# Tile 1's x is split on ScalarE and VectorE, and two weight pieces earlier, in a nine-expert MoE and adapter kernel

## What is computed

```python
# layer 0: eight routed experts and one shared expert (D=128, F=512)
g = einsum('bsd,edf->ebsf', x, Wg);  u = einsum('bsd,edf->ebsf', x, Wu)
expert_outs = einsum('ebsf,efd->ebsd', silu(g) * u, Wd)
shared = einsum('bsf,fd->bsd', silu(x @ Sg) * (x @ Su), Sd)
x = x + (1 - sg) * einsum('be,ebsd->bsd', gates, expert_outs) + sg * shared
# layer 1: an adapter chosen by the sequence's language, and a layer norm
h = relu(x @ W1[lang] + b1[lang])
y = x + h @ W2[lang] + b2[lang]
x = x + layernorm(y) * gamma[lang] + beta[lang]
```

## Time and profile before

| | |
|---|---|
| median of 3 runs | 296.86 us (296.78 to 297.94) |
| the profiled execution, its own time | 297.13 us |
| its span in the profile | 295.3 us |
| granted TensorE clock, mean | 0.996 |
| PE busy | 290.9 us, 99% |
| DVE busy | 267.9 us, 91% |
| ACT busy | 231.0 us, 78% |
| POOL busy | 18.8 us, 6% |

### The profile page before, as it was taken

The page is one execution under the profiler, slowest core; times in us unless marked ns, Lnnn a source line. Parts: engine busy times, 40 slices in busy tenths (PEclk is TensorE's granted clock), DMA queues, the critical chain, the costliest instruction groups (busy, mean ns, idle before and its releaser), DMA issues.

```text
span 295.3 us, 5098 instructions
## 1 busy us (share of the span) xinstructions
PE 290.9 (99%) x1515; PEld 145.7 (49%) x1515; DVE 267.9 (91%) x584; ACT 231.0 (78%) x515; POOL 18.8 (6%) x32
## 2 busy tenths in 40 slices
PE   8999999999999999999999999999999999999995
PEld 4444444444444444444444444444444444588883
DVE  4999999998989898988989999999999999977795
ACT  6998878788878787877897788887878876667771
POOL 3200201100000000000001010001100011000011
PEclk9999999999999999999999999999999999999998
DMA  7973110244000000000011001010001110000001
GB/s 205 373 322 109 51 66 20 60 119 114 3 2 0 2 0 0 0 2 1 1 23 25 18 9 39 12 25 21 18 0 39 26 19 10 2 36 3 0 2 36
DMA packets 17940, 13.39 MB, mean 45 GB/s; under 512 B 11486, under 2 KB 15994, under 8 KB 17914
## 3 DMA queue, kind: packets, MB, share of 16 engines
q1 hardware_dynamic: 17482, 12.86, 14.5%
q10 hardware_dynamic: 432, 0.21, 0.2%
HBM read 11.23 MB, written 1.05 MB: 42 GB/s over the span
## 4 chain that ended last, share of the span: by engine, by line
PE 98%; DVE 1%; POOL 0%; POOLq 0%; issue 0%; DVEq 0%
PE up_ps L445 11%; PE gate_ps L396 10%; PE moe_ps L468 10%; PE moe_ps L471 10%; PE up_ps L437 10%; PE moe_ps L469 10%; PE up_ps L440 10%; PE gate_ps L397 10%; PE gate_ps L402 10%; PE moe_ps L512 1%; PE adapt_ps L480 0%; DVE w_lo L689 0%; PE gate_ps L411 0%; PE moe_ps L452 0%; PE x_ps L497 0%; PE gate_ps L414 0%
## 5 line engine op out<-in xcount | busy, mean ns | idle before, releaser
L588 ACT ACTIVATE silu<-gate_ps 128x512 f32<-128x512 f32 (+1 forms) x160 | 88.5, 553 | 46.1 <-PE gate_ps L402 44.4
L705 DVE SCALAR_TENSOR_TENSOR hidden<-silu,up_ps 128x512 f32<-128x512 f32 (+1 forms) x160 | 101.2, 633 | 19.7 <-PE up_ps L445 12.0
L711 DVE TENSOR_TENSOR h_lo<-hidden,h_hi 128x512 f16<-128x512 f32 (+1 forms) x159 | 103.8, 653 | 0.2
L593 ACT ACTIVATE h_hi<-hidden 128x512 f16<-128x512 f32 (+1 forms) x159 | 92.4, 581 | 8.9 <-DVE hidden L705 8.1
L445 PE MATMUL up_ps<-gx_hi,w_lo 128*128 128x512 f16 (+1 forms) x160 | 57.2, 358 | 0.1
L437 PE MATMUL up_ps<-gx_hi,w_hi 128*128 128x512 f16 (+1 forms) x160 | 57.3, 358 | 0.0
L440 PE MATMUL up_ps<-gx_lo,w_hi 128*128 128x512 f16 (+1 forms) x160 | 57.2, 358 | 0.0
L469 PE MATMUL moe_ps<-h_hi,w_lo 128*128 128x512 f16 (+1 forms) x159 | 56.9, 358 | 0.0
L468 PE MATMUL moe_ps<-h_hi,w_hi 128*128 128x512 f16 (+1 forms) x159 | 56.9, 358 | 0.0
L471 PE MATMUL moe_ps<-h_lo,w_hi 128*128 128x512 f16 (+1 forms) x159 | 56.9, 358 | 0.0
L396 PE MATMUL gate_ps<-x_hi,w_hi 128*128 128x512 f16 (+1 forms) x158 | 56.5, 358 | 0.0
(11 more groups left out here) (95 smaller groups left out, 154.7 us busy)
## 6 DMA issues: line engine op xcount, KB each, us to landing
w_full<-weights SPq DMA_DIRECT2D x8, 768.0 KB, 9.0
affine_sb<-affine SPq DMA_DIRECT2D x16, 128.0 KB, 2.9
x_full<-xT SPq DMA_DIRECT2D x3, 256.0 KB, 8.4
x<-x_blocks SPq DMA_DIRECT2D x48, 16.0 KB, 1.8
out_dram<-result SPq DMA_DIRECT2D x3, 256.0 KB, 2.0
w_full<-weights SPq DMA_DIRECT2D x4, 128.0 KB, 3.2
w_full<-w2b SPq DMA_DIRECT2D x24, 16.0 KB
w_full<-weights SPq DMA_DIRECT2D x1, 256.0 KB, 3.9
```

What stands on the lines that cost most here:

```text
L588: nc.scalar.activation(silu_slot(n), gate_ps[n % 2][:, 0:STEPS[n][4]], ACT.Silu, scale=1.0 / W_SCALE).then_inc(silu_ready, 1)
L593: nc.scalar.activation(h_slot(h_hi, n), hidden_slot(n), ACT.Copy).then_inc(h_hi_ready, 1)
L705: nc.vector.scalar_tensor_tensor(out=hidden_slot(n), in0=silu_slot(n), scalar=HIDDEN_RESCALE * (W_SCALE if n < WHOLE_STEPS else 1), in1=up ...
L711: nc.vector.tensor_tensor(h_slot(h_lo, n), hidden_slot(n), h_slot(h_hi, n), ALU.subtract).then_inc(h_lo_ready, 1)
```

## The change

x of tile 1 is no longer split by GpSimd. ACT makes its `x_hi` in step 1, after two gx_hi and ahead of silu(2); DVE makes its `x_lo` in step 2, after the low part of piece 4 and ahead of h_lo(1). PE waits for `x_lo_ready` in place of `x_rest_ready` ahead of gate(4). The high and low parts of piece 3 are made ahead of silu(0) and hidden(0) in place of behind them. GpSimd makes the coefficients of experts 1 to 7 directly after those of expert 0, as soon as their gates are loaded, and then splits tiles 2 and 3 as before.

```diff
-X_AFTER = {1: 3, 2: lo_count(2, 2), 3: lo_count(3, 2)}
+X_AFTER = {2: lo_count(2, 2), 3: lo_count(3, 2)}
...
-                if t > 0 and e == 0 and f == 0:
-                    pe.wait_ge(x_rest_ready, t)
+                if t == 1 and e == 0 and f == 0:
+                    pe.wait_ge(x_lo_ready, 3)
+                if t > 1 and e == 0 and f == 0:
+                    pe.wait_ge(x_rest_ready, t - 1)
...
                 if n == 0:
                     first_weight_hi(2)
+                    first_weight_hi(3)
                 silu_of(n)
-                if n == 0:
-                    first_weight_hi(3)
                 if n in (1, 2):
                     gated_x_hi(1, 2 * n - 2)
                     gated_x_hi(1, 2 * n - 1)
+                if n == 1:
+                    nc.scalar.activation(cols(x_hi, 1, N), cols(x_full, 1, N), ACT.Copy).then_inc(x_hi_ready, 1)
...
                 if n == 0:
                     first_weight_lo(2)
+                    first_weight_lo(3)
                 hidden_of(n)
                 for j, (_, _, _, at) in enumerate(JOBS):
                     if n == at:
                         moe_out(j)
-                if n == 0:
-                    first_weight_lo(3)
...
                 if n == 2:
                     first_weight_lo(4)
+                    dve.wait_ge(x_hi_ready, 3)
+                    nc.vector.tensor_tensor(cols(x_lo, 1, N), cols(x_full, 1, N), cols(x_hi, 1, N),
+                                            ALU.subtract).then_inc(x_lo_ready, 1)
...
-            for t in range(1, TILES):
+            pool.wait_ge(gates_loaded, 16)
+            nc.gpsimd.tensor_tensor(coef[:, B:(NE - 1) * B].rearrange("p (e b) -> p e b", b=B),
...
+                                    ALU.mult).then_inc(coef_ready, 1)
+            for t in range(2, TILES):
                 pool.wait_ge(x_loaded[t - 1], 16)
-                if t > 1:
-                    pool.wait_ge(w_lo_ready, X_AFTER[t])
+                pool.wait_ge(w_lo_ready, X_AFTER[t])
                 nc.gpsimd.tensor_copy(cols(x_hi, t, N), cols(x_full, t, N)).then_inc(x_rest_hi_ready, 1)
-                pool.wait_ge(x_rest_hi_ready, t)
-                if t == 1:
-                    pool.wait_ge(w_lo_ready, X_AFTER[t])
+                pool.wait_ge(x_rest_hi_ready, t - 1)
                 nc.gpsimd.tensor_tensor(cols(x_lo, t, N), cols(x_full, t, N), cols(x_hi, t, N),
                                         ALU.subtract).then_inc(x_rest_ready, 1)
```

More of the change, by code:

```diff
@@ L879, in _ @@
             nc.gpsimd.tensor_scalar(coef[:, (NE - 1) * B:], shared_in, X_SCALE, None, ALU.mult)
-            for t in range(1, TILES):
+            pool.wait_ge(gates_loaded, 16)
+            nc.gpsimd.tensor_tensor(coef[:, B:(NE - 1) * B].rearrange("p (e b) -> p e b", b=B),
+                                    gates_in[:, 2 * B:].rearrange("p (e b) -> p e b", b=B),
+                                    rest[:, :].rearrange("p (o b) -> p o b", o=1).to_broadcast([P, NE - 2, B]),
+                                    ALU.mult).then_inc(coef_ready, 1)
+            for t in range(2, TILES):
                 pool.wait_ge(x_loaded[t - 1], 16)
-                if t > 1:
-                    pool.wait_ge(w_lo_ready, X_AFTER[t])
+                pool.wait_ge(w_lo_ready, X_AFTER[t])
                 nc.gpsimd.tensor_copy(cols(x_hi, t, N), cols(x_full, t, N)).then_inc(x_rest_hi_ready, 1)
-                pool.wait_ge(x_rest_hi_ready, t)
-                if t == 1:
-                    pool.wait_ge(w_lo_ready, X_AFTER[t])
+                pool.wait_ge(x_rest_hi_ready, t - 1)
                 nc.gpsimd.tensor_tensor(cols(x_lo, t, N), cols(x_full, t, N), cols(x_hi, t, N),
                                         ALU.subtract).then_inc(x_rest_ready, 1)
[L890 to L895, removed]
             nc.gpsimd.memset(ident[:, :], 0.0).then_inc(ident_zeroed, 1)
```

## The result

The changed kernel takes 297.77 us (median of 22 runs, 297.45 to 298.15), the kernel before 296.75 us (22 runs, 296.59 to 297.94): 1.02 us more, a ratio of 1.0030 with a 95% interval of 1.0025 to 1.0036. That is inside the 0.5% that the prediction took as no change, and inside its range, but it is nearly three times the +0.37 of its sum. So the question is where the other 0.65 us comes from.

What follows compares the result with a forecast made beforehand. The prediction took PE, busy 99% of the span, as the bound. Its terms -0.22 (hole in up(2)) and +0.59 (wait for x_lo) summed to +0.37 us, taking the median 296.86 to 297.2; range 296.5 to 298.2.

Steps and rivals of the forecast that it cites:

- the +0.37 of its sum: Whole kernel: 0.22 us gained in up(2) and 0.59 us lost ahead of gate(4), together +0.37 us.
- the deciding mechanism: DVE ahead of gate(4): x_lo of tile 1 runs 11.04 to 11.72, so PE idles 0.59 us.
- 0.68 for x_lo: On DVE: the subtraction for tile 1's x_lo takes 0.68 us, like h_lo of the same shape and types.
- 0.62 for x_hi: On ACT: the copy for tile 1's x_hi takes 0.62 us, like h_hi of the same shape and types.
- PE's 0.06: Ahead of gate(4): PE goes on 0.06 us after DVE ends x_lo, as seen in up(2).
- "Cost: nothing" for piece 3 ahead of silu(0): On ACT: piece 3 lands at 5.8, its split runs 5.90 to 6.31 in idle time before silu(0) at 6.52.
- Rival D: Piece 3 lands at 6.6 or later, delaying silu(0) and hidden(0); up to +0.59 us (297.5); chance 0.67 shared with forecast.
- rival B: GpSimd's coefficients collide with DVE's gx_lo at 8.61; x_lo ends up to 0.44 us later, 297.7 us; chance 0.15.
- the term -0.22: In up(2): PE's wait for piece 3's low part goes, third matmul at 8.81 instead of 9.03, 0.22 us gained.
- Rival C: The idle gap ahead of gate(4) drops PE to its slower pace; up to 2.6 us more, 299.8 us; chance 0.05.
- A: At gate(4): x_lo is in time and only the 0.22 us gain is left, 296.6 us; chance 0.1.

Runs made afterwards that it cites:

- x half alone: The changed kernel with weight piece 3 split where it was before, behind silu(0) and hidden(0); tile 1's x stays on ACT and DVE: 297.70 us, ratio 1.0025.

## Why the prediction was right and where it was wrong

*Right: the deciding mechanism.* x_lo, where DVE's order puts it, is late for gate(4), and PE idles. In the second profile of the changed kernel the rows are the predicted ones: hidden(2) at 9.30 (9.31), x_lo at 11.02 (11.04), gate(4) at 11.76 (11.78), the time of that execution 297.50 (297.5). Moving x_lo takes the loss away: 0.53 with the first place, and the rest of what can be told with the other two. The 0.68 for x_lo, 0.62 for x_hi and PE's 0.06 held.

*Wrong: "Cost: nothing" for piece 3 ahead of silu(0).* The step took the median landing of four loads, 3.2 us, for the last of the four, and called it there at 5.8. In the profile that it read, it had landed 3.3 after its issue; in the first one of the changed kernel 3.9, at 6.56. The slack ahead of silu(0) is 0.3, and what goes beyond it arrives at gate(4) undiminished (5.17 to 5.20 from silu(0)). Rival D had the late landing, and its condition (landing at 6.6 or later) is met nearly exactly, but it was given no chance of its own and its price went another way: it let the slip bring back the hole in up(2), up to +0.59 in all. The hole stayed away, and the slip came to x_lo through silu(0), silu(2) and hidden(2): +0.79 between the two first profiles. On the median it is some 0.26: 297.77 less 1.83 around the span less 283.9 gives gate(4) at 12.04, against the predicted 11.78 (an estimate, not measured by itself). That the landing counts is shown by the load moved both ways (-0.37 and +0.8).

*Wrong: the sum carried over to the median.* The prediction worked out +0.37 for the profiled execution and added it to 296.86, as if the typical execution of the changed kernel would again be shorter than the profiled one by 0.27. In the kernel before this surplus lay ahead of gate(4), in PE's slow start and in the hole. In the changed kernel gate(4) waits for x_lo, and a PE that is early there only waits longer. How little comes through is seen in two profiles: with piece 3 early PE ran at the 2.4 GHz pace from 4.26 on, and gate(4) started at 11.73; with x_lo one place earlier the pace rose at about 5.2, and gate(4) would have started at 11.65 with x_lo in its old place (10.31 + 0.60 + 0.74, an estimate). Both are within 0.11 of the 11.76 that came with a slow start until 5.9. The changed kernel itself has no profile with a fast start, so this step is in part argued. The typical gate(4) of the kernel before is 296.75 - 1.83 - 283.9 = 11.02 (an estimate like the 12.04 above), 0.39 earlier than in its first profile. 0.39 + 0.37 + 0.26 is 1.02, the measured difference, but it must be, since both ends come from the medians: the split says where the loss lies if the two estimates hold, and does not prove it.

That 297.77 lies inside the range is owed to its width. The upper bound was made from rival B and from the spread of three runs, and neither made the loss.

*Mis-sized: the term -0.22.* The place and the cause held: with GpSimd idle the low part of piece 3 took 0.42 (x half alone), with only the end of a cast beside it 0.48 (GpSimd's subtraction later), and the hole was gone both times. But its size was that of one execution, in which tile 1's x landed early; in the other it was 0.08, and taking only this away changed nothing measurable.

*Rival B* had its condition met and was harmless: the gates landed 4.4 after their issue in both profiles of the changed kernel, 0.8 later than the prediction had it. In the second profile the coefficients (8.54 to 8.96) lay beside the two gx_lo, which took 0.81 for 0.60; the 0.2 went into DVE's wait for up(2). *Rival C* did not come: behind the lost 0.91 matmuls follow each other at 0.22 (the 2.4 GHz level), and the mean granted clock is 1.0. *A* would have needed what only moving x_lo gave.

## What to carry to other kernels

A new job on a hand-ordered engine has to be placed by its deadline, not behind the jobs that are there: here moving one subtraction three places forward took away the loss, as far as it could be told. Where a chain that does not follow the bounding engine takes over, price it from its own start to its own end, and set it against the typical time of the other, not against one execution. And a wait on a load must not be put in front of work that others wait for unless the latest landing seen in several profiles, not a median of other loads in one, leaves room.

## What was not expected of the hardware

In the eleven profiles in which the loads are issued in the same order and at the same times, piece 3 (128 KB, fourth of the weight pieces in SP's queue) landed 3.1 to 3.9 us after its issue, and tile 1's x (256 KB) 3.7 to 4.8. The spread is within one program too: 3.3 and 3.8 for piece 3 in the two profiles of the kernel before, 3.9 and 3.5 in those of the changed one.

PE's pace at the start differs as much, though PE does the same ahead of it (eight matmuls of 512 columns from 0.78 on). Two matmuls of 256 columns took 0.39 to 0.43 (the 1.2 GHz level) until about 5.9 us in the first profile of the kernel before, and 0.22 to 0.23 (2.4 GHz) from 4.27 on in the second. The granted clock of this stretch is given as 1.00 in both, so it does not show the slow pace; only the starts of the matmuls do. In the second profile PE then waited in up(0), mostly for low parts of DVE, so that of the 0.8 that it was ahead 0.2 were left at up(1). Why the landings and the pace differ between executions was not tried.

Beside GpSimd, the end of a DVE instruction with two SBUF inputs follows the end of GpSimd's. The low part of piece 3 (0.42 when alone) ended 0.28 behind GpSimd's subtraction in the first profile of the kernel before, 0.27 behind its cast in the second, and 0.28 behind its cast (8.51 against 8.23) with the subtraction later. A pair of gx_lo ended 0.15 behind GpSimd's coefficients twice (10.24 against 10.09, and 10.40 against 10.25). The prediction had reckoned with the whole 0.42 behind GpSimd's end, which is 0.14 too much.
